# Two transformer-like layers on one core: the first experts and the attention behind them in one block, and the attention's operands prepared by 128 features of a batch

## The reference

```python
x = x + _L0_xattn_ref(ctx_512, _layernorm(x), W0, a_self0, a_neigh0, b0, W1, a_self1, a_neigh1, b1)
x = x + _L0_ffn_ref(_layernorm(x), gate, gate_up_proj, down_proj)          # 32 experts, top 4
x = x + _L1_xattn_ref(_layernorm(x), ctx_512, ctx_512)
x = x + _L1_ffn_ref(_layernorm(x), w_cls, bias, w_gate_up, w_down)         # 32 experts + 32 empty, top 8
```

```python
qh = q.reshape(B, S, KV, G, D).transpose(0, 2, 3, 1, 4)    # B=4, S=512, KV=8 key heads, G=4 query heads each, D=16
kh = k.reshape(B, S, KV, D).transpose(0, 2, 1, 3)          # k = v = ctx_512, (4, 512, 128)
scores = jnp.einsum('bkgsd,bktd->bkgst', qh, kh) / scale
weights = jax.nn.softmax(scores, axis=-1)
out = jnp.einsum('bkgst,bktd->bkgsd', weights, vh)
```

## Time and profile before

| | us |
|---|---|
| median of 3 runs | 2109.56 (2109.5 to 2125.61) |
| the profiled execution | 2110.66 |
| its span, first to last instruction | 2108.9 |
| PE busy | 1788.2 (85%) |
| DVE busy | 1388.2 (66%) |
| ACT busy | 1059.5 (50%) |
| POOL busy | 918.2 (44%) |

### The profile page before, as it was taken

How to read it: one execution, slowest core, us unless ns; L and a number is a source line. 1 busy time by engine, 2 the same in 40 slices (tenths; PEclk the granted TensorE clock), 3 DMA queues, 4 the chain that set the end, 5 groups by cost and what they waited for, 6 DMA issues and landing times. The chain is left out here.

```text
span 2108.9 us, 32488 instructions
## 1 busy us (share of the span) xinstructions
PE 1788.2 (85%) x9679; PEld 1016.9 (48%) x9679; DVE 1388.2 (66%) x2786; ACT 1059.5 (50%) x2135; POOL 918.2 (44%) x991
## 2 busy tenths in 40 slices
PE   4689877898447999999994599999996539999997
PEld 2344443444244555555552133333332538888885
DVE  5887877878585665655653687778783865455553
ACT  5588777888333333333331377777776512222222
POOL 5466676668203555555552241541111014444442
PEclk8699988999777999999997599999999759999999
DMA  5111121111354879989665643333222618999893
GB/s 150 56 41 41 57 84 61 41 41 41 128 168 103 178 185 237 232 181 232 146 116 102 121 124 72 89 87 82 64 58 62 252 49 228 232 233 236 229 233 65
DMA packets 194352, 270.93 MB, mean 128 GB/s; under 512 B 86956, under 2 KB 111500, under 8 KB 193164
## 3 DMA queue, kind: packets, MB, share of 16 engines
q1 hardware_dynamic: 150364, 168.23, 27.2%
q0 software_dynamic: 38544, 97.02, 22.5%
q10 hardware_dynamic: 5280, 3.67, 0.6%
HBM read 199.20 MB, written 69.17 MB: 127 GB/s over the span
## 5 line engine op out<-in xcount | busy, mean ns | idle before, releaser
L291 POOL TENSOR_TENSOR g_near<-g_mask,g_tb 128x512 f32<-128x512 f32 x256 | 322.2, 1279 | 99.8 <-DVE g_emin L545 98.8
L2096 DVE TENSOR_REDUCE a_negmax<-a_m 128x2 f32<-128x1024 f32 x256 | 304.3, 1221 | 85.6 <-PE a_m L1882 85.5
L1969 ACT ACTIVATE a_prob<-a_s 128x512 f32<-128x512 f32 x512 | 274.8, 595 | 90.6 <-PE a_s L1892 89.3
L1464 PE MATMUL f_gu_bank<-f_wgu,f_xT 128*128 x768 | 265.8, 489 | 2.9 <-ACT f_xT L1512 2.9
L1258 PEld LDWEIGHTS s_gu_bank<-s_xT,s_wgu 128*128 128x128 f32 x2048 | 240.3, 193 | 31.8 <-issue 27.5
L374 PE MATMUL g_pt<-g_ident,g_p 128*128 128x128 f32 x1024 | 173.7, 299 | 89.4 <-DVE g_pT L554 84.2
L1426 POOL DMA_INDIRECT out<-f_y,f_ids x96 | 151.7, 1580 | 209.7 <-DMA out<-f_y,f_ids 167.6
L1258 PE MATMUL s_gu_bank<-s_xT,s_wgu 128*128 128x128 f32 x2048 | 240.9, 276 | 1.6 <-ACT s_xT L1288 1.6
L475 ACT ACTIVATE g_p<-g_e,g_emin 128x512 f32<-128x512 f32 x256 | 183.4, 716 | 97.2 <-DVE g_emin L545 96.5
L374 PEld LDWEIGHTS g_pt<-g_ident,g_p 128*128 128x128 f32 x1024 | 122.3, 150 | 219.7 <-DVE g_pT L554 146.5
L1464 PEld LDWEIGHTS f_gu_bank<-f_wgu,f_xT 128*128 128x128 f32 x768 | 146.3, 191 | 126.1 <-issue 49.3
(11 more groups left out here) (296 smaller groups left out, 2766.3 us busy)
## 6 DMA issues: line engine op xcount, KB each, us to landing
s_wgu<-in_L_ffn_w_gate_up SPq DMA_DIRECT2D x32, 1024.0 KB
f_wgu<-in_L_ffn_gate_up_proj SPq DMA_DIRECT2D x32, 768.0 KB
s_wd<-in_L_ffn_w_down SPq DMA_DIRECT2D x32, 512.0 KB
g_tb<-neighbours SPq DMA_DIRECT2D x8, 1536.0 KB
f_wd<-in_L_ffn_down_proj SPq DMA_DIRECT2D x32, 384.0 KB
a_qT<-q_parts SPq DMA_DIRECT2D x64, 192.0 KB, 3.4
q_parts<-a_part SPq DMA_DIRECT2D x16, 384.0 KB, 4.0
g_tb<-neighbours SPq DMA_DIRECT2D x8, 512.0 KB
```

The source lines that it names most:

```text
L291: pool.tensor_tensor(near[:, n % LAG, :], mask[slot][:, local % NT, :], t_all[k % SLOTS][:, local // NT, :], ALU.add).then_inc(near_ready, 1)
L1464: last = nc.tensor.matmul(gu_bank[j % TR][:, 0:F], xT[j % TR][:, c, :], wgu_flat[:, bass.ds(place_of[j] + c * F, F)], start=(c == 0), stop ...
L1969: nc.scalar.activation(prob[n][:, :], bank_of("score", G, n)[:, :], ACT.Exp).then_inc(p_ready, 1)
L2096: V.tensor_reduce(negmax[k % RING][:, 2 * half:2 * half + 2, head], m_bank[i % RING][:, :, :], X_AXIS, ALU.max, negate=True).then_inc(m_re ...
```

## The change

Five things, all between the first experts and the end of the attention:

1. The experts and the attention share one `Block` and one `stage_semaphores`. No meeting of the engines stands between them any more. PE waits for the last `f_y` of ACT; POOL waits for the last scatters and then raises one semaphore, `experts_done`; SP and ACT wait for it before they load tokens. The attention's tiles take the place of the experts' in SBUF, and their order is changed (the tiles that are written first stand further on); the identity of the router is used on.
2. The context of batch 0 is loaded and its keys are turned, split and subtracted by PE, ACT and DVE without waiting for `experts_done`; the rest of the context is loaded later, after the first units.
3. A unit of queries is now 128 features (two groups' queries) of all 512 tokens of a batch, in place of 128 tokens with all features. A store's contiguous run in HBM is 1024 bytes (512 numbers), before 256. SP reads the queries of a group as soon as the one unit that holds them is stored. The normalised tokens have two places of four tiles, before one.
4. Five units come first (keys 0 and four of queries), before eight. 15 are late: keys and four units of queries for each of the batches 1 to 3, in the groups 0 to 4, 8 to 12 and 16 to 20. POOL normalises two tiles in each of the groups 7, 8, 13 and 14.
5. On SP, a late unit's store stands at the head of the group's body, and the eight key DMAs of the next batch go out three, three and two, in the second to fourth group.

```diff
-def open_ffn(nc, tokens, gate, gate_up, down, K, pre):
+def open_ffn_and_attention(nc, tokens, gate, gate_up, down, K, pre, ctx_dram, q_parts, k_parts):
...
-        open_experts(nc, tokens, gate_up, down, x_rows, kept, n_tiles, RE, pre + "_")
+        with nc.Block() as block:
+            y_ready, landed = open_experts(nc, tokens, gate_up, down, x_rows, kept, n_tiles, RE, pre + "_", block, sem)
+            stack.close()
+            attention(nc, tokens, ctx_dram, q_parts, k_parts, block, lambda name: sem("a_" + name), y_ready, n_tiles, landed, ident)
...
-    units = [("keys", 0)] + [("tokens", t) for t in range(NT)] + [("keys", b) for b in range(1, B)]
+    units = [("keys", 0, 0)] + [("queries", 0, c) for c in range(DC)]
     FIRST = len(units)
-    units += [("tokens", t) for t in range(NT, TT)]
-    late_group = list(range(NT)) + list(range(KV, KV + 2 * NT))
+    for b in range(1, B):
+        units += [("keys", b, 0)] + [("queries", b, c) for c in range(DC)]
+    late_group = [G for G in range(GROUPS - KV) if G % KV <= DC]
     late_at = {G: i for i, G in enumerate(late_group)}
+    norms_at = {7: (8, 9), 8: (10, 11), 13: (12, 13), 14: (14, 15)}
...
-        part = sb("part", [P, PLACES, DC, PARTS, P], BF16)
+        part = sb("part", [P, PLACES, PARTS, N], BF16)
+        xn = sb("xn", [P, 2, NT, D])
...
             def load_q(G, k):
-                if g == 0 and b > 0:
-                    for r in range(PLACES):
-                        sp.wait_ge(stored[r], 16 * (2 + b))
+                if g % 2 == 0:
+                    u = place_of["queries", b, g // 2]
+                    sp.wait_ge(stored[u % PLACES], 16 * (u // PLACES + 1))
...
+            sp.wait_ge(experts_done, 1)
             load_tokens(0, NT // 2, 0)
-            load_tokens(NT, NT, 2)
-            sp.wait_ge(consts, 4)
+            sp.wait_ge(consts, 3)
             load_keys(0, len(K_PART))
-            for u in range(3):
-                store(u)
+            store(0)
+            load_tokens(NT, NT, 2)
             for r in range(len(K_PART)):
                 load_keys(0, r)
-            for u in range(3, 5):
-                store(u)
-            for t in range(NT):
-                sp.wait_ge(stored[(1 + t) % PLACES], 16 * ((1 + t) // PLACES + 1))
+            store(1)
             load_q(0, 0)
             load_q(1, 1)
-            for u in range(5, FIRST):
+            for u in range(2, FIRST):
                 store(u)
...
             def body(G, k, ahead):
+                if G in late_at:
+                    store(FIRST + late_at[G])
...
-                if b < B and 0 <= step < 4:
-                    load_keys(b, 2 * step)
-                    load_keys(b, 2 * step + 1)
-                if G in late_at:
-                    store(FIRST + late_at[G])
+                if b < B and 0 <= step < 3:
+                    for r in range(3 * step, min(3 * step + 3, len(K_PART) + 1)):
+                        load_keys(b, r)
...
         def _(pe):
-            pe.wait_ge(consts, 4)
+            pe.wait_ge(y_ready, y_count)
...
         def _(act):
             act.dma_start(ctx_sb[:, 0:NT, :], ctx_dram[0, :, :].rearrange("(t p) f -> p t f", p=P)).then_inc(ctx_in[0], 16)
-            act.dma_start(tok[:, NT // 2:NT, :], tokens[NT // 2 * P:N, :].rearrange("(t p) d -> p t d", p=P)).then_inc(tok_in[1], 16)
-            act.dma_start(ctx_sb[:, NT:TT, :], ctx_dram[1:B, :, :].rearrange("b (t p) f -> p (b t) f", p=P)).then_inc(ctx_in[1], 16)
             first_part(0)
             second_part(0)
+            act.wait_ge(experts_done, 1)
+            act.dma_start(tok[:, NT // 2:NT, :], tokens[NT // 2 * P:N, :].rearrange("(t p) d -> p t d", p=P)).then_inc(tok_in[1], 16)
...
             second_part(FIRST - 1)
+            act.dma_start(ctx_sb[:, NT:TT, :], ctx_dram[1:B, :, :].rearrange("b (t p) f -> p (b t) f", p=P)).then_inc(ctx_in[1], 16)
...
         def _(pool):
-            pool.memset(ident[:, :], 0.0).then_inc(chain_p, 1)
+            for semaphore, count in landed:
+                pool.wait_ge(semaphore, count)
+            pool.sem_inc(experts_done, 1)
+            third_part(0)
             pool.memset(one_rows[:, :], 1.0).then_inc(consts, 1)
```

More of the change, by code:

```diff
@@ L1325, in _, with open_experts @@
                     dve.wait_ge(act_ready, j + 1)
-def open_experts(nc, tokens, gate_up, down, x_rows, kept, n_tiles, RE, pre):
+def open_experts(nc, tokens, gate_up, down, x_rows, kept, n_tiles, RE, pre, block, sem):
     NE, D, F = gate_up.shape
@@ new lines, in _, with gather, landed @@
+        @block.gpsimd
+        def _(pool):
+            last_row = pool.to_reg(T + 2 * P - 1)
+            def gather(j):
+                if j >= XR:
+                    pool.wait_ge(act_ready, j - XR + 1)
+                pool.indirect_dma_start(out=row[j % XR][:, :], out_offset=None, in_=x_rows,
+                                        in_offset=bass.IndirectOffsetOnAxis(ap=ids[:, j:j + 1], axis=0),
+                                        bounds_check=last_row).then_inc(row_in[j % XR], 16)
+            def landed(j):
+                return 16 * (j // 2)
+            for j in range(AHEAD):
+                gather(j)
+            for j in range(n_tiles):
+                if j + AHEAD < n_tiles:
+                    gather(j + AHEAD)
+                pool.wait_ge(y_ready, j + 1)
+                if j >= 2:
+                    pool.wait_ge(added[j % 2], landed(j))
+                if j in (1, 2):
+                    pool.wait_ge(added[(j - 1) % 2], landed(j + 1))
+                if j > 2:
+                    new = pool.value_load(fresh[0:1, j:j + 1], min_val=0, max_val=16)
+                    pool.wait_ge(added[(j - 1) % 2], new + landed(j - 1))
+                    pool.sem_inc(turns_pool, 1)
+                pool.indirect_dma_start(out=tokens, out_offset=bass.IndirectOffsetOnAxis(ap=ids[:, j:j + 1], axis=0),
+                                        in_=y[j % YR][:, :], in_offset=None, compute_op=ALU.add,
+                                        bounds_check=last_row).then_inc(added[j % 2], 16)
@@ L1568 @@
+    return y_ready, [(added[i], 16 * (n_tiles // 2)) for i in range(2)]
 K_PART = (0, 0, 0, 1, 1, 1, 2)
@@ L1573, with attention @@
 ROWS_ALL = PAIR_ROWS + PARTS
-def attention(nc, tokens, ctx_dram, q_parts, k_parts):
+def attention(nc, tokens, ctx_dram, q_parts, k_parts, block, sem, y_ready, y_count, landed, ident):
     B, N, CF = ctx_dram.shape
@@ L1715, in part_of, with xn_of @@
         def part_of(u, j):
-            return part[:, u % PLACES, :, j, :]
+            return part[:, u % PLACES, j, :]
         def left_of(u):
-            return left[:, u % PLACES, :].rearrange("p (c s) -> p c s", c=DC)
+            return left[:, u % PLACES, :]
+        def xn_of(t):
+            return xn[:, t // NT % 2, t % NT, :]
         def by_head(row):
```

1162 lines of the change are left out of this document (561 added, 601 removed).

## The result

| | median us | fastest to slowest | profiled execution | its span |
|---|---|---|---|---|
| before | 2109.53 | 2107.25 to 2125.61 (4 runs) | 2110.66 | 2108.9 |
| changed | 2085.74 | 2083.16 to 2087.82 (4 runs) | 2085.85 | 2084.0 |

The ratio of the times is 0.9867, with a 95% interval of 0.984 to 0.9894: faster by 1.3%. The forecast was 2081 with a range of 2072 to 2093. One execution of an experiment's kernel (keys late) took 4567.55 us, in a slow state; it counts in no ratio here.

A forecast was written before the change was run, and what follows sets the result against it. PE bounds the attention's groups; the joint is a chain with an empty stretch. Terms -20.9 - 13.1 + 1.4 + 4.0 = -28.6 against the profiled 2110.66 give 2082, as a median 2081 us; range 2072 to 2093.

The forecast's parts named there:

- Empty stretch: Between experts' last scatter and attention: no engine busy, no DMA; one shared block lets tokens be asked for 8.4 us earlier.
- Tokens to the first store: At the joint: tokens asked for at 1141.2, first store of queries issued at 1156.1, before at 1166.88.
- Read to first product: At the joint, first read of queries to first product of the maxima: 4.3 us as before, reaching 1164.4.
- rival D: At the joint: remaining 768 KB of context meets the first query reads, head start lost to traffic; 2087 to 2091, chance 0.08.
- Groups: Attention's groups: no PE waits for rows of ones in groups 6, 14, 22, 13.1 us less; 15 late units, 1.4 more.
- the second sign of being wrong: Forecast wrong if a wait that the key stall hid came out in groups 6, 14 and 22.
- Give-back: Attention's end: POOL must still end its block there, so 4.0 us of its closing surplus return.
- Case A: The forecast itself, with POOL's closing cost returning at the attention's end: 2081 (2077 to 2088), chance 0.42.
- B: Attention's end: nothing is given back there; 2077 (2072 to 2083), chance 0.25.
- C: At the joint: POOL pays its closing cost at once, delaying its first work behind the scatters; 2083 to 2088, chance 0.12.
- E: Groups gain nothing, as another wait takes the place of the ones, 13 back; 2092 to 2096, chance 0.08.
- F: Late groups: SP's store waits for POOL's parts, maxima come late, PE stands and its clock falls; slower, 2165, chance 0.05.

The follow-up runs named there:

- keys late: The changed kernel with the next batch's key reads again two in a group over four groups, rows of ones last; ratio 0.9935 (0.9911 to 0.996).

## Why the prediction was right, and where it wasn't

- **Empty stretch, -8.4.** Right in the sum, 8.3 to 8.9, and partly by luck: its two parts were off in opposite directions. The meetings and clearings are 1.9, not 3.2, and POOL's drain 6.4, not 5 to 6. The trace of before had the drain as an instruction of its own, 6.44 us long; I had inferred it from idle times, and doubled what one closing costs at the attention's end (1.6), which the two clearings together hardly exceed.
- **Tokens to the first store.** Right: 15.5 us against 14.9 by the steps. The first read follows 3.8 behind the store (said 4.0).
- **Read to first product, 4.3.** Off by 1.6 (5.93). This is rival D, at half of its price and inside the forecast: by the Trainium skill (DMA: Bandwidth & Descriptors, "Issuing engines are not separate DMA queues") ACT's DMAs and SP's share the engines, and the trace agrees: 4.34 to 4.36 in the three profiles whose context isn't under way, 5.59 and 5.93 in the changed kernel's two, where it is. Sum of this part: -20.0 for -20.9. For the stores' longer runs in HBM I took nothing, and no run here separates them.
- **"The keys made during the joint cost nothing and bring little."** The first half is right, the second wrong. Without them the first maxima come 9.2 to 9.7 later, half of the 20. The sum had them, since it left the key reads out of the way, but the sentence spoke only of when keys 0 are ready and so sold the largest piece of the joint that a run isolates as a detail.
- **Groups, -13.1 and +1.4.** Groups 14 and 22 are at 12.23 for 12.2, and a group with a late unit at 12.71. Group 6 is wrong: 14.1 said (17.27 less my own 3.0 would be 14.3), 16.81 measured, and 15.18 where the clock holds. PE's wait for the ones, 2.98, went; its wait for ACT stayed at 1.71; and two waits for DVE's maxima, 0.42 and 0.31, came out, which the long wait had hidden. So with the clock held the group gained 2.1. That is the second sign of being wrong that I had named, in this one group. The lower clock behind ACT's wait then takes 1.6 of it.
- **Give-back, +4.0.** Case A, right: 4.2 to 4.4. With the drain at its true size the working gives it: 6.4 less the 2.0 of SP's store. B is out (the debt waited 450 us, and less POOL's last addition it was as large as before), and C too (POOL's first instruction came 3.23 behind its last scatter). The reason I gave, that it goes with the number of DMAs, holds for order of size alone.
- **E and F** didn't happen in the changed kernel: but for group 6 no wait took the place of the ones, and PE never waited for a unit's store. What F feared, PE standing for the maxima's rows, shows in small in two of the experiments' profiles (1.41 and 0.85, both ahead of group 4), and there it isn't a store that waits for POOL, but DMAs that land late.

The sum said -28.6, the executions -24.8. Of the 3.8 between them 0.9 lie before the first score (the read's 1.6 and 0.6 up to the first store, less 1.1 by which the tokens were asked for ahead of the forecast's 1141.2), 1.9 in the groups (group 6 gave 0.5 in place of 3.0; group 0 was 0.5 shorter, which the sum didn't have), 0.4 at the attention's end and 0.6 behind it.

## What to carry to other kernels

A cost that an engine pays when it closes a block is not saved by merging blocks; it moves to the next end. What is saved are the barriers and clearings (1.5 to 1.9 us here), what the next end hides of the cost (2 of 6.4), and above all the time until work may begin: here the keys are made early. Where such a debt is left, pay it in a gap of the same engine. And a long wait hides short ones behind it: when it is taken out, look at that place again, and at what the clock does behind the waits that stay.

## What the runs showed of the hardware

- POOL's DRAIN behind its DMAs is not a wait for something that passes with time. For the 192 DMAs of the first experts it took 6.44 us right behind them with POOL idle, and 7.22 to 7.23 in group 21 or at the end of the attention, 320 to 450 us later, where POOL's last addition of 0.72 runs inside it. Where nothing was owed it took 0.82 with such an addition in it. It took 3.49 for the 124 DMAs and 3.82 for the 128 of the second experts, and 0.37 for their last 4. For the three large ones that is 0.028 to 0.034 us for each DMA, if gathers and scatters count alike. But with plain scatters it was 8.45, and the graph stage's 33 plain DMAs of POOL left 0.40 in all, so the number of DMAs isn't the whole law; what else counts stays open.
- The DRAIN doesn't first sit out the landing of a DMA that is on its way: begun at the last scatter's issue, it ended 9.0 us behind it; begun behind the landing, 11.7.
- PE's clock fell to its lower level behind a wait of 1.71 in group 6 in 2 of 9 profiles (granted 0.73 over the next 6.4 us) and held in 7, with the same instructions ahead of it. Behind the 2.5 to 3.1 for the ones it fell in groups 14 and 22 each time (0.57 to 0.65), and in group 6 it held before the change (2.98) and fell with the keys late (2.86). It is worth 1.6 us in a group, in one and the same kernel.
